# Expert choice of each first half spread over more turns, softmax of two by a tangent, and the second attention's first turn moved into the tile loop

## The reference

```python
x = x + 0.5 * ffn(layernorm(x))       # 128 -> 512 -> 128, ternary weights, relu
x = x + attn0(layernorm(x))           # 16 heads of 64, causal, rmsnorm and gates
x = x + 0.5 * ffn(layernorm(x))
x = x + 0.5 * moe(layernorm(x))       # 8 experts, 2 per token
x = x + attn1(layernorm(x))           # 16 heads of 64, causal
x = x + 0.5 * moe(layernorm(x))

def moe(X):
    logits = X @ Wg + bg
    topv, topi = top_k(logits, 2)
    w = softmax(topv)                  # two weights per token
    xs = X[:, :, None, :] * w[..., None]
    out = X
    for e in range(8):
        h = silu(xs @ W1[e]) * (xs @ W3[e])
        out = out + where(topi == e, h @ W2[e], 0).sum(over the 2 choices)
    return out
```

## Time and profile before

| | us |
|---|---|
| median of 3 runs | 997.93 (995.46 to 999.84) |
| the profiled execution | 999.04 |
| its span in the trace | 997.3 |
| first attention's turns 1 to 35, then first expert stage | to about 377, to about 523 |
| second attention, then second expert stage | to about 849, to 997 |

### The profile page before, as it was taken

The page is one execution under the profiler, slowest core; times in us unless marked ns, Lnnn a source line. Parts: engine busy times, 40 slices in busy tenths (PEclk is TensorE's granted clock), DMA queues, the critical chain, the costliest instruction groups (busy, mean ns, idle before and its releaser), DMA issues.

```text
span 997.3 us, 33895 instructions
## 1 busy us (share of the span) xinstructions
PE 895.7 (90%) x13160; PEld 641.2 (64%) x13160; DVE 800.0 (80%) x2394; ACT 688.1 (69%) x1187; POOL 738.7 (74%) x690
## 2 busy tenths in 40 slices
PE   5779999999999879899996899999999976799994
PEld 3447677676776656676763577677767755476663
DVE  6768998888889887887764799898888898786773
ACT  6668888879877645666763778767867763566663
POOL 6579989889988735676664998977878874467772
PEclk9899999999999988999996999999999998799997
DMA  5111010110030001122111000000000000112232
GB/s 154 45 43 32 16 45 16 32 45 3 3 97 12 3 3 38 54 45 90 44 38 48 3 3 3 13 3 2 13 3 3 14 2 7 38 46 53 91 73 82
DMA packets 21118, 33.79 MB, mean 34 GB/s; under 512 B 4578, under 2 KB 10466, under 8 KB 20964
## 3 DMA queue, kind: packets, MB, share of 16 engines
q1 hardware_dynamic: 14544, 19.29, 6.2%
q0 software_dynamic: 5888, 12.07, 4.8%
q10 hardware_dynamic: 532, 0.27, 0.1%
HBM read 22.44 MB, written 9.18 MB: 32 GB/s over the span
## 4 chain that ended last, share of the span: by engine, by line
PE 65%; DVE 20%; ACT 5%; issue 5%; POOL 2%; DMA 1%; ACTq 0%; SPq 0%; POOLq 0%; DVEq 0%
PE ps L1578 9%; PE ps L1763 8%; PE ps L1580 8%; PE ps L1579 8%; DVE arena L1242 4%; PE ps L1793 4%; PE ps L1998 4%; PE ps L1730 3%; PE ps L1795 3%; PE ps L1794 3%; PE ps L1803 2%; PE ps L2011 2%; PE ps L2010 2%; PE ps L1741 2%; PE ps L2012 2%
## 5 line engine op out<-in xcount | busy, mean ns | idle before, releaser
L735 POOL TENSOR_TENSOR arena<-arena 128x1024 f16<-128x1024 f32 x190 | 345.2, 1817 | 100.7 <-ACT arena L929 89.9
L921 ACT ACTIVATE arena<-ps,lift 128x1024 f32<-128x1024 f32 (+1 forms) x192 | 186.7, 972 | 88.6 <-PE ps L1773 83.4
L1242 DVE CUSTOM_DVE_ANT_0 arena<-ps,mask_qk 128x512 bf16<-128x512 f32 (+3 forms) x512 | 224.4, 485 | 24.8 <-PE ps L1730 23.7
L1763 PE MATMUL ps<-arena 64*128 64x512 f16 (+3 forms) x1536 | 149.9, 301 | 9.4 <-ACT arena L921 6.1
L782 POOL DMA_INDIRECT arena<-x_rows,arena x92 | 91.1, 990 | 69.0 <-PE ps L1973 35.8
L1793 PE MATMUL ps<-arena 128*128 128x65 f16 x1280 | 133.9, 197 | 0.7 <-DVE arena L1266 0.7
L1794 PE MATMUL ps<-arena 128*128 128x64 f16 x1280 | 133.2, 195 | 0.0
L1795 PE MATMUL ps<-arena 128*128 128x65 f16 x1280 | 132.9, 195 | 0.0
L1793 PEld LDWEIGHTS ps<-arena 128*128 128x128 f16 x1280 | 119.1, 99 | 9.2 <-DVE arena L1266 0.9
L790 POOL DMA_INDIRECT y_rows<-arena x92 | 91.5, 994 | 40.5 <-issue 23.7
L1794 PEld LDWEIGHTS ps<-arena 128*128 128x128 f16 x1280 | 119.6, 100 | 0.3 <-issue 0.3
(11 more groups left out here) (269 smaller groups left out, 2753.2 us busy)
## 6 DMA issues: line engine op xcount, KB each, us to landing
stage<-in_L_ffn_W SPq DMA_DIRECT2D x4, 1024.0 KB, 5.4
arena<-y_rows SPq DMA_DIRECT2D x16, 256.0 KB, 3.5
x_rows<-XN SPq DMA_DIRECT2D x8, 256.0 KB, 2.2
arena<-x_rows,arena POOLq DMA_INDIRECT x92, 2.7
y_rows<-arena POOLq DMA_INDIRECT x92
stage<-in_L_attn_Wkv SPq DMA_DIRECT2D x2, 512.0 KB, 7.8
out_x<-X SPq DMA_DIRECT2D x4, 256.0 KB, 2.6
X<-in_L_attn_tokens SPq DMA_DIRECT2D x3, 256.0 KB, 5.3
```

Of the source, the lines that this page charges most:

```text
L735: g.tensor_tensor(PL[:, b, :, cols], P32[:, :, cols], PH[:, b, :, cols], ALU.subtract).then_inc(s_pl, 1)
L921: a_.activation(P32[:, :, UNIT_AT[u]:UNIT_AT[u] + UNIT_W[u]], ps[:, 4:6, 0:UNIT_W[u]], ACT.Exp, bias=lift[:]).then_inc(s_ex_p, 1)
L1242: v_.tensor_tensor_reduce(masked[:, x, 0:w], ps[:, 2 + x, at:at + w], mask_qk[:, CH - w:CH], 1.0, NEG, ALU.add, ALU.max, accum_out=MX[:, i ...
L1763: mm(ps[:, 4 + x, at:at + w], keys, queries, start=(n_ == 0 and part == 0), stop=False)
```

## The change

1. The choice of a first half is cut into more pieces, over turns 30 to 35. `chosen_half` loses its one-hot sets to `hot_half`; `places_half` becomes `counts_half` (behind the maxima of turn 32, and it first copies TensorE's ranks out of PSUM) and `ranks_half` (end of turn 32); `sorted_half` becomes `rows_half` and `places_half`; `weights_half` (small instructions, now at the end of turn 33) leaves its two products to `weight_sets` (turn 35). TensorE's parts go ahead of the output projection.
2. The same pieces for a second half take 11 passes where they took 7. In `moe(0)` they start at pass 11, and what was carried in passes 0 to 8 comes one or two passes later.
3. The two weights come from a tangent: with h = tanh(d/2), they are (1-h)/2 and (1+h)/2.
4. The tiles' buffers move behind the attention's q, k and v in the arena. So GpSimd can run `attention_set` and `step_rows(1)` in pass 30 of `moe(0)`, and turn 0 of the second attention (the projections of item 0, in banks 6 and 7) runs in pass 44 on TensorE, ScalarE and VectorE. The additions of expert results (`x_moe`) for chunks 1 to 3 move from turns 0 to 2 to turns 1 to 3.

```diff
-        used[0] = 2048
+        used[0] = walk_at
         XG = carve([XRING, D], F32)
...
+        def qv_bank(a, p):
+            return 6 if (a, p) == (1, 0) else 0
...
 # GpSimd
-                    if a == 1 and t < NCH - 1:
-                        x_moe(t + 1)
+                    if a == 1 and 1 <= t < NCH:
+                        x_moe(t)
...
+                    if u == 30:
+                        attention_set()
+                        step_rows(1)
...
             moe(0)
-            attention_set()
             base_add(4, 0, bout[:])
...
 # ScalarE
-                a_.activation(wts[:, 1, :], wts[:, 0, :], ACT.Exp).then_inc(s_r_exp, 1)
+                a_.activation(wts[:, 1, :], wts[:, 0, :], ACT.Tanh, scale=0.5).then_inc(s_r_exp, 1)
...
+                    if t == 44:
+                        attention(1, range(1))
...
-            attention(1)
+            attention(1, range(1, TURNS))
...
 # VectorE, body(t) of attention
                     if t == TURNS - 1:
                         index_half(a, 0)
+                        weight_sets(a, 0)
                     if o is not None:
                         turned_low()
                     if t == TURNS - 3:
-                        sorted_half(a, 0, 1)
+                        rows_half(a, 0, 1)
+                        places_half(a, 0, 1)
...
                     if late_k(a, t):
                         k_low()
+                    if t == TURNS - 4:
+                        counts_half(a, 0)
...
+                    if t == TURNS - 6:
+                        chosen_half(a, 0)
                     if t == TURNS - 5:
-                        chosen_half(a, 0)
+                        hot_half(a, 0)
                     if t == TURNS - 4:
-                        places_half(a, 0)
-                run_items(body)
-                homes_half(a, 0)
-                stats(2 + 3 * a, 3)
+                        ranks_half(a, 0)
+                    if t == TURNS - 3:
+                        weights_half(a, 0)
+                    if t == TURNS - 1:
+                        homes_half(a, 0)
+                        stats(2 + 3 * a, 3)
...
-                step(v_.tensor_scalar(wts[:, 0, :], wts[:, 1, :], 1.0, None, ALU.add))
-                step(v_.reciprocal(wts[:, 2, :], wts[:, 0, :]))
-                step(v_.tensor_tensor(wts[:, 3, :], wts[:, 1, :], wts[:, 2, :], ALU.mult))
+                v_.tensor_scalar(wts[:, 2, :], wts[:, 1, :], -0.5, 0.5, ALU.mult, ALU.add)
+                step(v_.tensor_scalar(wts[:, 3, :], wts[:, 1, :], 0.5, 0.5, ALU.mult, ALU.add))
...
 # VectorE, routed(m, t): 7 passes become 11
                 if t == 0:
                     chosen_half(m, 1)
+                    hot_half(m, 1)
                 if t == 1:
-                    places_half(m, 1)
+                    counts_half(m, 1)
                 if t == 2:
-                    sorted_half(m, 1, 1)
+                    ranks_half(m, 1)
...
+                if t == 9:
+                    tiles_half(m, 1)
+                if t == 10:
                     homes_half(m, 1)
...
 # TensorE, body(t) of attention
                     if o is not None:
                         turn_outputs()
+                    if t == TURNS - 4:
+                        pe.wait_ge(s_v_lo, base + ITEMS)
+                        ranks_half(a, 0)
...
+                    if t == TURNS - 2:
+                        sums_half(a, 0)
+                    if t == TURNS - 1:
+                        weights_half(a, 0)
                     if o is not None:
                         project_out()
...
 # TensorE, carried(0, t)
-                    if t == 0:
+                    if t == 1:
                         down(1, 2)
...
-                    routed(0, t - 9)
+                    routed(0, t - 11)
...
+                    if t == 44:
+                        attention(1, range(1))
```

More of the change, by code:

```diff
@@ L177, in macaron_block @@
         PCOLS = 1280
+        walk_at = used[0]
         P32 = carve([2, PCOLS], F32)
@@ L482, in seq_of, with run_items @@
             return j // PAIRS
-        def run_items(body):
-            for t in range(TURNS):
+        def run_items(body, turns):
+            for t in turns:
                 body(t)
@@ L716, in _, with attention @@
             head_low(2)
-            def attention(a):
+            def attention(a, turns=range(TURNS)):
                 def body(t):
@@ L736, in body @@
                                             ).then_inc(s_pl, 1)
-                    if t == 0:
+                    if a == 0 and t == 0:
                         step_rows(a)
@@ L755, in body @@
                         rstd_of(*STATS[a][t])
-                run_items(body)
+                run_items(body, turns)
             def carried(m, u):
@@ L1748, in scores @@
                             pe.wait_ge(s_nm_sb, j + 1)
+                            if a == 1 and s == 0:
+                                pe.wait_ge(s_y_sb, ETILES)
                             pe.wait_ge(s_q_lo, j + 1)
@@ L1944, in carried @@
                         second_turned(t // 2 - 12)
-                    if t == 41:
+                    if t == 42:
                         pe.wait_ge(s_w_lo, 8)
                         turned_x(4, 0)
+                    if t == 44:
+                        attention(1, range(1))
                 else:
```

161 lines of the change are left out of this document (87 added, 74 removed).

## The result

| | before | after |
|---|---|---|
| median of 7 runs, us | 997.93 (995.46 to 999.99) | 991.83 (990.63 to 992.24) |
| the profiled execution, us | 999.04 | 990.63 |
| its span, us | 997.3 | 988.6 |

The ratio is 0.994, with a 95% interval of 0.9927 to 0.9954; a second measurement beside other kernels gave 990.92 us and 0.9926 (0.9911 to 0.994). So the change wins some 7 us and not the 18 of the forecast; 980.0 and the whole range 969 to 990 were too low.

A forecast was written before the change was run, and what follows sets the result against it. TensorE was taken as the bound (busy 895.7 of 997.3 us), only idle and half-clock time winnable; -5.7 - 5.1 - 6.5 + 0.3 - 0.5 + 0.5 - 1.5 = -18.5 gave 980.5, stated as 980.0 median; range 969 to 990.

The forecast's parts named there:

- Routing in the tile loop: Expert stages' routing passes: table loads go and VectorE's work spreads over more passes; -5.7 us in `moe(0)`, -5.1 in `moe(1)`.
- Rival A: Routing: stalls only spread and only the loads go, -2.6 us each; 985.6 us; chance 0.14.
- The seam: Into the second attention: memset and turn 0 move into the tile passes, turn 1 follows the last tile; -6.5 us.
- the added sums of chunks 2 and 3: Second attention, turns 2 and 3: GpSimd adds 2.6 us each beside the score work; priced at +0.6 us.
- Pass 30 and `down(1, 2)`: GpSimd's set-up in pass 30 delays gathers and scatters, +0.3 us; the matmuls moved to pass 1 join the path, +0.5.
- Last turns of the first attention: Turns 30 to 35: chosen half split, weights earlier, counts in turn 32's idle 2.05 us; -0.5 us (-4 to +3).
- three of them may wait for one of its instructions each, and the evacuation comes up to 1.8 us late: First attention, turn 32: of the counts' ten instructions, three may wait for GpSimd, delaying the evacuation up to 1.8 us.
- Last turns of the second attention: Choice pieces lie on the path; splitting the chosen half, earlier weights and counts win; -1.5 us (-4 to +3).
- VectorE is the bound there: Second attention's last turns: VectorE busy 9.25 of 10 us near turn 30, so the choice pieces lie on the path.
- the prediction's three signs of being wrong: TensorE's idle time falls under 10 us; tile passes 45 to 48 take over 4 us each; last turns get longer.
- rival D: Turns 30 to 33: small VectorE pieces each lose the port to a GpSimd instruction, 28 us; 1008 us; chance 0.02.

The follow-up runs named there:

- before_tanh: The kernel before with only the tangent for the weights and the two instructions making both weights, all else in its old place; 992.12 us, ratio 0.9936.
- counts_late: The changed kernel with the first half's counts at turn 32's end on VectorE, ahead of the ranks; 1033.76 us on the slower chip, ratio 1.0036.
- ranks_counts_late: As counts_late, with TensorE's rank matmuls also moved, behind the output projection at turn 32's end; 1027.32 us on the slower chip, ratio 0.9981.
- port_free: The changed kernel with GpSimd's casts and subtractions of items 29 and 30 on 8 columns per unit; 1021.36 us on the slower chip, ratio 0.9916.
- counts_psum: The changed kernel with the small tables of the first half's counts and ranks in PSUM in place of SBUF; 982.40 us, ratio 0.9841.
- x_moe_early: The changed kernel with expert sums of chunks 1 and 2 in turn 1, chunk 3 in turn 2; 1034.48 us on the slower chip, ratio 1.0031.
- mended: The changed kernel with the edits of x_moe_early and ranks_counts_late together; 981.13 us, ratio 0.9832.

## Why the prediction was wrong

- **Routing in the tile loop: right.** -5.25 and -4.7 for -5.7 and -5.1. The eleven passes took 30.31 us where the sum said 30.3. The second stage came out 0.4 short of its term. Rival A (only the loads go) falls: spreading alone won 2.1 and 2.7 (before_tanh against the changed kernel).
- **The seam: right in mechanism, one term failed.** Turn 1 took 7.7 us, as worked out from the earlier trace rows, and the stage won 7.7. But I put the added sums of chunks 2 and 3 at +0.6, from GpSimd's share of a steady turn. Turn 3 isn't steady: the same engine has a norm's instructions there, and the whole of the 2.5 us came onto the path. The average hid the one turn that was full.
- **Pass 30 and `down(1, 2)`: right**, nothing and +1.0 for +0.3 and +0.5.
- **Last turns of the first attention: wrong** by 3 us. The step that failed is "three of them may wait for one of its instructions each, and the evacuation comes up to 1.8 us late". Five waited, for 4.6 us in sum, and the evacuation L1149 came 4.5 us later behind item 30's Exp: every instruction of the chain waits for the one ahead, so after each loss the next meets GpSimd's next instruction. And I had named the evacuation as what is queued behind the counts, but not L1149, for which TensorE's output projection waits (the 6.00 us above). counts_late took 3.8 us off by that place alone.
- **Last turns of the second attention: wrong** by 4.8 us, of the same sort. I took "VectorE is the bound there", from the earlier trace rows, for a slot in which shorter pieces win. The sum of the choices, now just ahead of turn 32 with TensorE's rank matmuls moved ahead of the second unit of scores, lost to GpSimd and held TensorE for 2.97 us; this move of TensorE's matmuls I hadn't priced at all. ranks_counts_late took 2.9 us off by it against counts_late, 1.8 against the changed kernel.

Two of the prediction's three signs of being wrong came true: TensorE's idle time fell by 3.3 us (101.6 to 98.3), not by 10, and the last turns got longer.

So rival D had the mechanism (small pieces that lose the port one after another), and I gave it 0.02 since I looked only at the size that would turn the sign. At a quarter of that size (7.8 us for 28) it took 40% of the 18.5. The Trainium skill (SBUF — State Buffer, "SBUF: two separate sides") says that the pair is held for a whole instruction and that the other side fully blocks. port_free and the ends of the rows, which lie within 0.09 us of each other, agree with it; and counts_psum, where all that changed is that one side lies in PSUM, with its limit to instructions in a two-port mode or with two SBUF inputs.

Open: why the tile passes take longer on one of the chips. ScalarE starts there up to 2.5 us late on inputs that are there, and the trace puts it down to nothing on this core ("remote"). TensorE's last matmul for this result ended at 952.29 (ScalarE, x_moe_early):

```profile
953.99 0.28 ACT L1103 ACTIVATE arena<-ps 128x128 f32<-128x128 f32 x1 [1.66 <-remote]
```

Neither the changed kernel nor the kernel before was profiled there; by x_moe_early's ratio of 1.0031 the change may be no gain on such a chip. The +1.0 us behind tile 10 of the second stage (0.7 in the second execution) is not looked into. Nor is it shown what sets the granted clock of turn 32, 0.74 of full speed before and 1.00 in mended (item 30's Exp to item 31's).

## What to carry to other kernels

Before a chain of small dependent instructions is moved on VectorE, lay GpSimd's rows of the same microseconds beside it: each link can lose up to one whole GpSimd instruction (here up to 2.1 us for one of 0.17), and idle time on VectorE is no slack where GpSimd fills it. Where it can't be moved, keep its tables in PSUM. And for each moved instruction list everything queued behind it and who waits for that, on TensorE as on VectorE; a share of busy time over a steady turn doesn't price a turn that carries extra work.

## What the hardware showed that I had not expected

- The kernel before took 3.3% longer on one chip (1030.97 us); in the four kernels profiled there the excess lay in the tile passes, from tile 0 on.
